# Probabilities times values of the cross attention: from fp32 matmuls to three fp16 products of high and low parts

## The chip, the cores and the metric

The kernel runs on one core of one Trainium2 chip. The metric is the device time of one execution in microseconds (us). Before the change two runs gave 828.41 and 826.72 us, a median of 827.57 us.

Five engines work side by side, each through its own instructions in order, and they wait for each other on semaphores. PE (TensorE) multiplies, DVE (VectorE) and ACT (ScalarE) read its results from PSUM, POOL (GpSimd) works between buffers in SBUF alone, and SP issues most of the DMAs.

## The reference

A decoder layer on x of 8 x 128 x 512: x plus self attention of the normed x (128 heads), plus cross attention of the normed result to a context of 8 x 128 x 512 (32 query heads, 8 key and value heads, head size 16, rotary positions), plus a base layer with eight gated low rank experts of the normed result. The change is in these lines of the cross attention:

```
v = jnp.repeat(v, N_REP, axis=1)
scores = jnp.einsum('bhqd,bhkd->bhqk', q, k) * scale
probs = jax.nn.softmax(scores, axis=-1)
ctx = jnp.einsum('bhqk,bhkd->bhqd', probs, v)
```

## The kernel before

The program spells out each engine's instructions by hand. Self attention fills the first three quarters of the span. The last quarter, from about 640 us, is the cross attention and the expert layer, written as one software pipeline over 32 **units**. A unit `u` is one of the 8 batches `b = u // 4` and one of four groups of 8 query heads `t = u % 4`. Every engine runs the same loop `for u in range(FIRST, ...)` with `b, r = (u + 1) // 4, (u + 1) % 4`. In step `u` of the loop the different parts of the pipeline work on different units:

- PE: `turn(u+2)` and `x_back(u-2)` (transposes, L1788 and L1839), then the long work of that step (below), then `x_rough(u+2)` (scores for the row maxima, L1798), `x_max_turn(u+1)`, `x_scores(u)` (scores by key, L1817) and `x_weigh(u-1)` (L1832), which multiplies the exponentials `XPT` with the values `xvz`. A column of ones beside the values gives the sums of the softmax.
- ACT: `turned_out(u+2)` (KQ, L1013), small reads of the step, `x_exps(u, 0)` (L1005), `x_out(u-1)` (OW, L1047), `x_exps(u, 1)`, and in the steps with r = 1 last the copy `query_high` (qst, L1055).
- DVE: the row maxima `x_max` (L1311), `x_outputs(u-1)` (division by the sums, L1321 and L1325), and the norms, gates and residual sums of the step.
- POOL: only a few pieces. In r = 0 it adds the bias (L810), in r = 1 it makes the low part of the queries (L817), in r = 2 it computes an inverse square root (L787, `inverse(1, ...)`) and spreads the keys (L828 to L831), in r = 3 another inverse square root (L787, `inverse(2, b - 1)`). This last one waits for the variance that DVE computes at the very end of its own step with r = 3 (`norm_stats(2, b - 1)`, L1288 to L1290). In six early steps POOL also makes low parts of weights (`split_low`, L798 and L801).

The long work on PE is the projection of the outputs in r = 3 (L1501, 12 matmuls) with a `norm_turn` (four transposes, L1849), the query projection in r = 0 (L1501, 12), the base layer and experts in r = 1 (L1740, 12, and L1747) with another `norm_turn`, and only the short gate product in r = 2 (L1501, 12 of 136 columns) with the transposes of the outputs (L1864). `XPT` has two buffers, picked by `u % 2`; the output of `x_weigh` goes to one PSUM bank.

The self attention already multiplies its probabilities in the way that the change brings to the cross attention: an fp16 copy `Ph` on ACT (L938), a low part `Pl` on POOL (L656), and 12 fp16 matmuls (L1654). `x_exps` and `x_weigh` of before are:

```
if u >= 2:
    act.wait_ge(s_xo, u - 1)
nc.scalar.activation(XPT[:, u % 2, h], PS[:, 4 + h, :], ACT.Exp).then_inc(s_ex, 1)
...
pe.wait_ge(s_ex, 2 * u + 2)
for g in range(2):
    for h in range(2):
        r = 32 * (2 * g + h)
        last = mm(PS[r:r + 32, o_bank(u), 0:2 * S], xvz[:, b, 2 * t + g, :], XPT[:, u % 2, h, 2 * g * S:2 * (g + 1) * S],
                  start=True, stop=True)
```

Of the kernel before, what the change touches and what calls it, by code (L numbers as in the profile page):

```python
# [7 lines left out]
F32 = mybir.dt.float32  # L8
F16 = mybir.dt.float16
# [5 lines left out]
P = 128  # L15
# [97 lines left out]
def build(nc, x, ctxT, pos, wdkr, wup, wqr, wo, xwq, xwkv, xwo, bw, ag, lb, bb, out):  # L113
    es = ExitStack()
    with es:
# [7 lines left out]
        def sb(name, shape, dt=F32):  # L123
            n = size[dt]
            for s in shape[1:]:
                n *= s
            at = top[0]
            top[0] = at + (n + 63) // 64 * 64
            return nc.alloc_sbuf_tensor_at(name, shape, dt, offset=at)
# [74 lines left out]
        assert top[0] <= os_at + 2 * GH * S * 4  # L204

        top[0] = end1 - 4 * KT * TOK * 2
        Pl = sb("Pl", [P, B, GH * S], F16)
        U = sb("U", [P, KT, TOK])
        SU = sb("SU", [P, TOK])
# [13 lines left out]
        CTh = sb("CTh", [P, KT, TOK], F16)  # L223
        CTl = sb("CTl", [P, KT, TOK], F16)

        top[0] = phase
        rt = sb("rt", [P, 2, DM])
        Wxh = sb("Wxh", [P, KT, DM], F16)
# [1 line left out]
        kst = sb("kst", [P, 2, NKV, 2, XROW], F16)  # L230
        assert top[0] <= wraw_at
        top[0] = wraw_at
        xvz = sb("xvz", [P, B, NKV, 32])
        assert top[0] <= w16_at
        top[0] = w16_at
        pn1 = sb("pn1", [P, 2, DM])
# [349 lines left out]
        def _(pool):  # L586
# [175 lines left out]
            for h in range(LATE, NH):  # L762
                p_low(job(h - 3))
                if h < TURN - 1:
                    late_rest(job(h).g + 1)
                if h == LATE:
                    values(G0 - 1, (G0 - 1) % 2)
                else:
                    late_values(job(h - 1))
                if h == TURN:  # L770
                    nc.gpsimd.memset(xvz[:], 0.0).then_inc(s_xvz, 1)
                if h == TURN + 1:
                    pool.wait_ge(s_kvo, B)
                    pool.wait_ge(s_xvz, 1)
                    nc.gpsimd.tensor_copy(xvz[:, :, :, 0:XVC], xv[:]).then_inc(s_xvz, 1)

            late_values(job(NH - 1))
            pool.wait_ge(s_q, 2 * NH)
# [12 lines left out]
            def split_low(n, k):  # L791
# [8 lines left out]
                pool.wait_ge(s_xw, done[0])  # L800
                nc.gpsimd.tensor_tensor(l, w, h, ALU.subtract).then_inc(s_xl, 1)  # L801

            for u in range(FIRST, LAST):
                b, r = (u + 1) // KT, (u + 1) % KT
                if r == 0 and 0 <= b - 2 < B:
                    v = b - 2
                    if v == 0:
                        pool.wait_ge(s_ffn, 80)
                    pool.wait_ge(n_xn[2], v + 1)
                    nc.gpsimd.tensor_tensor(xs[:, v, :], xs[:, v, :], bias[:], ALU.add).then_inc(s_xb, 1)  # L810
                if r == 1 and 0 <= b + 1 < B:

                    v = b + 1
                    pool.wait_ge(s_qst, 2 * v + 1)
                    q = qr[:].rearrange("p (h d) -> p h d", d=XD_)
                    part = [qst[:, v % 2, :, XD_ * i:XD_ * (i + 1)] for i in range(3)]
                    nc.gpsimd.tensor_tensor(part[2], q, part[0], ALU.subtract).then_inc(s_xqr, 1)  # L817
                if r == 2:
                    inverse(1, b + 2)
                if r == 2 and 0 <= b + 2 < B:  # L820

                    v = b + 2
                    if v >= 2:
                        pool.wait_ge(s_xt, KT * (v - 1))
                    pool.wait_ge(s_kvr, v // 4 + 1)
                    k = krc[:, v, :, None, :].to_broadcast([P, NKV, 2, XD_])
                    part = [kst[:, v % 2, :, :, XD_ * i:XD_ * (i + 1)] for i in range(3)]
                    nc.gpsimd.tensor_copy(part[0], k).then_inc(s_kst, 1)  # L828
                    nc.gpsimd.tensor_copy(part[2], k)
                    pool.wait_ge(s_kst, 2 * v + 1)  # L830
                    nc.gpsimd.tensor_tensor(part[1], k, part[0], ALU.subtract).then_inc(s_kst, 1)  # L831
                for n, k in LOWS_AT.get(u, ()):
                    split_low(n, k)
                if r == 3:
                    inverse(2, b - 1)

        @block.scalar
        def _(act):
# [161 lines left out]
            def x_exps(u, h):  # L1000
                if 0 <= u < NU:
                    act.wait_ge(s_st, 2 * u + h + 1)
                    if u >= 2:
                        act.wait_ge(s_xo, u - 1)
                    nc.scalar.activation(XPT[:, u % 2, h], PS[:, 4 + h, :], ACT.Exp).then_inc(s_ex, 1)  # L1005

            def turned_out(u):
                if 0 <= u + 2 < NU:
# [49 lines left out]
            for u in range(FIRST, NU):  # L1058
# [16 lines left out]
                x_exps(u, 0)  # L1075
                x_out(u - 1)
                x_exps(u, 1)
                if r == 1 and 0 <= b + 1 < B:
                    query_high(b + 1, 0)
                if u == FIRST + 2:  # L1080
# [411 lines left out]
        def _(pe):  # L1492
# [329 lines left out]
            def x_weigh(u):  # L1822

                b, t = u // KT, u % KT
                if 1 <= u < NU - 1:
                    pe.wait_ge(s_xon, u)
                pe.wait_ge(s_ex, 2 * u + 2)
                pe.wait_ge(s_xvz, 2)
                for g in range(2):
                    for h in range(2):  # L1830
                        r = 32 * (2 * g + h)
                        last = mm(PS[r:r + 32, o_bank(u), 0:2 * S], xvz[:, b, 2 * t + g, :], XPT[:, u % 2, h, 2 * g * S:2 * (g + 1) * S],  # L1832
                                  start=True, stop=True)
                last.then_inc(s_xo, 1)

            def x_back(u):
# [172 lines left out]
```

## Time and profile before

| What | Value |
|---|---|
| median of the runs | 827.57 us |
| the profiled execution, its own time | 826.78 us |
| its span in the trace | 824.5 us |
| mean granted clock of PE over the span | 0.998 |
| PE, DVE, ACT, POOL busy | 793.0, 628.6, 582.7, 590.9 us |

The span is what the trace covers, from its first to its last record; the execution's own time is 2.3 us longer. Busy time is a sum over the whole span. What an engine's time is worth in one stretch has to be read from that stretch: which engine waits there, and for whom. The names in the trace are the program's, with the line of the source (L1832 is `x_weigh`, L1005 is `x_exps`). An instruction of PE on fp32 operands has two records in the trace.

### The profile page before, as it was taken

How to read it: one execution, taken by the hardware profiler on the slowest of the kernel's cores; microseconds unless marked ns; L12 is line 12 of the kernel's file. 1: busy time of each engine (PE TensorE's matmuls, PEld its weight loads, DVE VectorE, ACT ScalarE, POOL GpSimd, SP SyncE). 2: the span in 40 equal slices, each digit the busy share in tenths (PEclk: the TensorE clock that was granted, in tenths of full speed). 3: DMA queues.
4: the chain of work that ended last, by engine and by line, in shares of the span. 5: the costliest groups of instructions: out<-in, count | busy, mean ns of one | idle time of the engine just before them, and what ended most of it. 6: DMA issues, size and time to landing. Idle time of an engine off the chain costs nothing.

```text
span 824.5 us, 17894 instructions
## 1 busy us (share of the span) xinstructions
PE 793.0 (96%) x5641; PEld 391.9 (48%) x5641; DVE 628.6 (76%) x1190; ACT 582.7 (71%) x1072; POOL 590.9 (72%) x535
## 2 busy tenths in 40 slices
PE   5999999999999999999999999999999899999987
PEld 3464444444444444444444444444444444555444
DVE  6766676676677788776788876778878888888766
ACT  8757777777777777777777777778765655666551
POOL 7967999999988888887888887878655634222111
PEclk9999999999999999999999999999999999999999
DMA  9344355533434333343333344352321000000001
GB/s 344 124 172 142 93 142 161 162 98 89 104 107 120 90 79 93 89 128 100 100 81 97 83 119 107 92 158 63 88 61 48 27 2 2 14 14 13 18 15 39
DMA packets 52176, 75.80 MB, mean 92 GB/s; under 512 B 10256, under 2 KB 34096, under 8 KB 51616
## 3 DMA queue, kind: packets, MB, share of 16 engines
q1 hardware_dynamic: 52128, 75.23, 32.8%
q8 instruction: 22, 0.36, 0.2%
q14 instruction: 26, 0.21, 0.1%
HBM read 38.69 MB, written 19.40 MB: 70 GB/s over the span
## 4 chain that ended last, share of the span: by engine, by line
PE 87%; DVE 4%; ACT 3%; issue 2%; SPq 2%; DMA 1%; POOL 0%; DVEq 0%; ACTq 0%
PE PS L1567 40%; PE PS L1639 7%; PE PS L1606 7%; PE PS L1640 7%; PE PS L1501 6%; PE PS L1654 5%; PE PS L1740 2%; PE PS L1832 2%; PE PS L1679 1%; PE PS L1798 1%; PE PS L1616 1%; PE PS L1688 1%; PE PS L1839 1%; PE PS L1817 1%; PE PS L1849 1%
## 5 line engine op out<-in xcount | busy, mean ns | idle before, releaser
L1567 PE MATMUL PS<-XTh,W 128*128 128x512 f16 x1024 | 346.0, 379 | 0.0
L656 POOL TENSOR_TENSOR Pl<-PR,Ph 128x512 f16<-128x512 f32 x254 | 285.8, 1156 | 28.4 <-ACT Ph L938 28.4
L931 ACT ACTIVATE PR<-PS 128x512 f32<-128x512 f32 x256 | 152.8, 597 | 131.7 <-PE PS L1640 124.9
L1125 DVE TENSOR_REDUCE mneg<-PS 128x4 f16<-128x512 f32 x256 | 171.6, 685 | 35.3 <-PE PS L1606 33.4
L1567 PE MATMUL PS<-XTl,W 128*128 128x512 f16 x512 | 193.6, 378 | 0.0
L1113 DVE SCALAR_TENSOR_TENSOR QS<-PS,QC 64x512 f16<-64x512 f32 x256 | 175.5, 685 | 20.8 <-ACT QC L848 16.7
L848 ACT ACTIVATE QC<-PS 64x512 f16<-64x512 f32 x256 | 150.7, 589 | 9.2 <-PE PS L1567 4.3
L1567 PEld LDWEIGHTS PS<-XTh,W 128*128 128x128 f16 x1024 | 96.6, 97 | 118.8 <-issue 25.9
L938 ACT ACTIVATE Ph<-PR 128x512 f16<-128x512 f32 x256 | 139.3, 617 | 0.0
L1606 PEld LDWEIGHTS PS<-KC,QC 112*128 112x128 f16 x1024 | 78.4, 97 | 63.5 <-issue 2.7
L1606 PE MATMUL PS<-KC,QC 112*128 112x128 f16 x1024 | 99.4, 219 | 0.9 <-ACT QC L848 0.8
L1639 PE MATMUL PS<-QC,KC 113*128 113x512 f16 x256 | 97.7, 382 | 1.3 <-DMA QC<-mT 1.2
L1640 PE MATMUL PS<-QS,KS 128*128 128x512 f16 x256 | 97.2, 380 | 0.0
L631 POOL TENSOR_TENSOR W<-Wraw,wscale 128x1024 f16<-128x1024 f32 x30 | 56.8, 1893 | 46.5 <-PE PS L1567 42.1
L1194 DVE TENSOR_SCALAR mT<-PS 16x128 f16<-16x128 f16 x64 | 13.6, 212 | 77.7 <-PE PS L1616 77.6
L1567 PEld LDWEIGHTS PS<-XTl,W 128*128 128x128 f16 x512 | 49.8, 97 | 46.3
L637 POOL TENSOR_TENSOR W<-Wraw,W 128x1024 f16<-128x1024 f32 x30 | 63.9, 2131 | 2.4
L787 POOL TENSOR_TENSOR rstd<-rstd,power 128x1 f32<-128x1 f32 x16 | 8.8, 553 | 74.3 <-DVE rstd L1290 74.3
L635 POOL TENSOR_TENSOR Wraw<-Wraw,wscale 128x1024 f32<-128x1024 f32 x30 | 56.7, 1891 | 0.2
L1200 DVE COPY OS<-PS 128x512 f32<-128x512 f32 x64 | 44.3, 692 | 4.1 <-PE PS L1654 2.2
L1311 DVE TENSOR_REDUCE xm<-PS 128x4 f16<-128x512 f32 x64 | 41.0, 683 | 2.0 <-PE PS L1798 2.0
L1654 PE MATMUL PS<-Ph,Vg 128*32 128x512 f16 x512 | 41.3, 383 | 0.0
(236 smaller groups left out, 1034.1 us busy)
## 6 DMA issues: line engine op xcount, KB each, us to landing
Wraw<-in_wqr SPq DMA_DIRECT2D x32, 512.0 KB, 4.8
QS<-QC SPq DMA_DIRECT2D x64, 256.0 KB, 3.2
head_outputs<-OS SPq DMA_DIRECT2D x256, 40.0 KB
q_content_parts<-stg SPq DMA_DIRECT2D x12, 256.0 KB, 2.9
k_content_parts<-stg SPq DMA_DIRECT2D x12, 256.0 KB, 3.1
QC<-q_content_parts SPq DMA_DIRECT2D x116, 24.0 KB
KC<-k_content_parts SPq DMA_DIRECT2D x29, 96.0 KB
xs<-in_x SPq DMA_DIRECT2D x8, 256.0 KB, 4.8
```

Of the source, the lines that this page charges most:

```text
L637: nc.gpsimd.tensor_tensor(Wl[:, par], Wraw[:, par], Wh[:, par], ALU.subtract).then_inc(s_ws, 1)
L656: nc.gpsimd.tensor_tensor(Pl[:, 4 * j.s + b], PR[:, b], Ph[:, 4 * j.s + b], ALU.subtract).then_inc(s_pl, 1)
L848: nc.scalar.activation(QC[0:RD, j.p, j.s, 2 * c + h, :], PS[RD * h:RD * (h + 1), bQ[c], :], ACT.Copy, scale=1 / WS).then_inc(s_qh, 1)
L931: nc.scalar.activation(PR[:, b, :], PS[:, bB[b % 2], :], ACT.Exp, scale=ATT_SCALE).then_inc(s_e, 1)
L938: nc.scalar.activation(Ph[:, 4 * j.s + b, :], PR[:, b, :], ACT.Copy).then_inc(s_ph, 1)
L1113: nc.vector.scalar_tensor_tensor(QS[0:RD, j.p, j.s, i, :], PS[RD * h:RD * (h + 1), bQ[c], :], 1 / WS, QC[0:RD, j.p, j.s, i, :], ALU.mult, ...
L1125: nc.vector.tensor_reduce(mneg[:, j.p, j.s, :, b], PS[:, bA[b % 2], :].rearrange("p (j k) -> p j k", j=GH), AX.X, ALU.max, negate=True).th ...
L1567: last = mm(PS[:, bQ[c], :], wt[:, j.w, k, c * P:(c + 1) * P], xt[:, k, sl], start=(i == 0), stop=(i == 3 * KT - 1))
L1606: last = mm(PS[:, bA[i % 2], h * S:(h + 1) * S], QC[0:MROW, j.p, j.s, h, i * S:(i + 1) * S], kc(j.k)[0:MROW, b * S:(b + 1) * S], start=Tru ...
L1639: mm(to, kc(j.k)[0:MROW + 1, b * S:(b + 1) * S], QC[0:MROW + 1, j.p, j.s, :, i * S:(i + 1) * S], start=True, stop=False)
L1640: mm(to, KS[:, b * S:(b + 1) * S], QS[:, j.p, j.s, :, i * S:(i + 1) * S], start=False, stop=True).then_inc(s_b, 1)
L1654: last = mm(PS[32 * b:32 * (b + 1), bO, :], Vg[:, j.p, part, 4 * j.s + b, :], probs[:, 4 * j.s + b, :], start=(n == 0), stop=(n == 2))
```

## The change

Only the product of probabilities and values in the cross attention is changed. ACT copies each half of the exponentials to fp16 (`XPh`, new function `x_highs`), POOL subtracts the copy from the original and writes the difference as fp16 (`XPl`, new function `x_lows`), and the values are kept as an fp16 pair in `xvz`, made once. `x_weigh` then adds three fp16 products, high by high, high values' low part by high, and low by high: 12 matmuls of 256 columns in place of 4 in fp32. PE waits for `XPl` only ahead of the third product. `x_exps(u)` now waits for the subtraction of unit u - 2 and no longer for its product.

```diff
-        xvz = sb("xvz", [P, B, NKV, 32])
+        xvz = sb("xvz", [P, 2, B, NKV, 32], F16)
...
+        XPh = sb("XPh", [P, 2, 2, REP * S], F16)
+        XPl = sb("XPl", [P, 2, 2, REP * S], F16)
...
-                    nc.gpsimd.tensor_copy(xvz[:, :, :, 0:XVC], xv[:]).then_inc(s_xvz, 1)
+                    nc.gpsimd.tensor_copy(xvz[:, 0, :, :, 0:XVC], xv[:]).then_inc(s_xvz, 1)
+                    pool.wait_ge(s_xvz, 2)
+                    nc.gpsimd.tensor_tensor(xvz[:, 1, :, :, 0:XVC], xv[:], xvz[:, 0, :, :, 0:XVC], ALU.subtract).then_inc(s_xvz, 1)
...
+            def x_lows(u):
+                if 0 <= u < NU:
+                    for h in range(2):
+                        pool.wait_ge(s_ph, 4 * NH + 2 * u + h + 1)
+                        if u == 0 and h == 0:
+                            pool.wait_ge(s_pv, NH)
+                        if u >= 2:
+                            pool.wait_ge(s_xo, u - 1)
+                        nc.gpsimd.tensor_tensor(XPl[:, u % 2, h], XPT[:, u % 2, h], XPh[:, u % 2, h], ALU.subtract).then_inc(s_pl, 1)
...
             for u in range(FIRST, LAST):
                 b, r = (u + 1) // KT, (u + 1) % KT
+                x_lows(u - 1)
...
                     if u >= 2:
+                        act.wait_ge(s_pl, pool_lows(NH - 1, 3) + 2 * (u - 2) + h + 1)
+                    nc.scalar.activation(XPT[:, u % 2, h], PS[:, 4 + h, :], ACT.Exp).then_inc(s_ex, 1)
+
+            def x_highs(u, h):
+                if 0 <= u < NU:
+                    act.wait_ge(s_ex, 2 * u + h + 1)
+                    if u >= 2:
                         act.wait_ge(s_xo, u - 1)
-                    nc.scalar.activation(XPT[:, u % 2, h], PS[:, 4 + h, :], ACT.Exp).then_inc(s_ex, 1)
+                    if u == 0 and h == 0:
+                        act.wait_ge(s_pv, NH)
+                    nc.scalar.activation(XPh[:, u % 2, h], XPT[:, u % 2, h], ACT.Copy).then_inc(s_ph, 1)
...
                 x_exps(u, 0)
                 x_out(u - 1)
                 x_exps(u, 1)
+                x_highs(u, 0)
+                x_highs(u, 1)
                 if r == 1 and 0 <= b + 1 < B:
                     query_high(b + 1, 0)
...
-                pe.wait_ge(s_ex, 2 * u + 2)
-                pe.wait_ge(s_xvz, 2)
-                for g in range(2):
-                    for h in range(2):
-                        r = 32 * (2 * g + h)
-                        last = mm(PS[r:r + 32, o_bank(u), 0:2 * S], xvz[:, b, 2 * t + g, :], XPT[:, u % 2, h, 2 * g * S:2 * (g + 1) * S],
-                                  start=True, stop=True)
+                pe.wait_ge(s_ph, 4 * NH + 2 * u + 2)
+                pe.wait_ge(s_xvz, 3)
+                for n, (probs, part) in enumerate(((XPh, 0), (XPh, 1), (XPl, 0))):
+                    if n == 2:
+                        pe.wait_ge(s_pl, pool_lows(NH - 1, 3) + 2 * u + 2)
+                    for g in range(2):
+                        for h in range(2):
+                            r = 32 * (2 * g + h)
+                            last = mm(PS[r:r + 32, o_bank(u), 0:2 * S], xvz[:, part, b, 2 * t + g, :],
+                                      probs[:, u % 2, h, 2 * g * S:2 * (g + 1) * S], start=(n == 0), stop=(n == 2))
```

How the new instructions stand among the old ones matters, since each engine keeps to its order. POOL in the second half of the cross attention, from the inverse square root of a step with r = 2 over r = 3, 0 and 1 to the next one of r = 2, before (a row is source line, operation, written tile <- read tiles, shape, and the semaphores waited for: `var_ready2` is the variance that DVE sends at the end of its step, `normed2` the normed rows, `xq_high` ACT's copy of the queries):

```order
L787 TENSOR_TENSOR rstd<-rstd,power 128x1 [waits var_ready1]
L828 CAST kst<-krc 128x16x16 [waits k_roped,kq_turned]
L829 CAST kst<-krc 128x16x16
L831 TENSOR_TENSOR kst<-krc,kst 128x16x16 [waits xk_parts]
L787 TENSOR_TENSOR rstd<-rstd,power 128x1 [waits var_ready2]
L810 TENSOR_TENSOR xs<-xs,bias 128x512 [waits normed2]
L817 TENSOR_TENSOR qst<-qr,qst 128x32x16 [waits xq_high]
```

and the same stretch of the change, where the source lines are shifted (`p_high` is ACT's copy of the exponentials):

```order
L795 TENSOR_TENSOR rstd<-rstd,power 128x1 [waits var_ready1]
L849 CAST kst<-krc 128x16x16 [waits k_roped,kq_turned]
L850 CAST kst<-krc 128x16x16
L852 TENSOR_TENSOR kst<-krc,kst 128x16x16 [waits xk_parts]
L821 TENSOR_TENSOR XPl<-XPT,XPh 128x512 [waits xo_ready,p_high] x2
L795 TENSOR_TENSOR rstd<-rstd,power 128x1 [waits var_ready2]
L821 TENSOR_TENSOR XPl<-XPT,XPh 128x512 [waits xo_ready,p_high] x2
L831 TENSOR_TENSOR xs<-xs,bias 128x512 [waits normed2]
L821 TENSOR_TENSOR XPl<-XPT,XPh 128x512 [waits xo_ready,p_high] x2
L838 TENSOR_TENSOR qst<-qr,qst 128x32x16 [waits xq_high]
L821 TENSOR_TENSOR XPl<-XPT,XPh 128x512 [waits xo_ready,p_high] x2
```

Each step now begins with two subtractions of the unit before, behind whatever POOL still had to do or to wait for in the step before: the pair of r = 0 stands behind the wait for `var_ready2`, the pair of r = 2 behind the wait for `xq_high`.

ACT from the score reads of a step with r = 1 to the read of KQ in r = 2, before:

```order
L998 ACTIVATE xmT<-PS 8x128 [waits xmax_in1,xmax_turned]
L1005 ACTIVATE XPT<-PS 128x512 [waits xo_ready,scores_by_key_ready]
L1047 ACTIVATE OW<-PS 128x256 [waits xo_turned,xo_ready]
L1005 ACTIVATE XPT<-PS 128x512 [waits xo_ready,scores_by_key_ready]
L1055 ACTIVATE qst<-qr 128x32x16 [waits kq_turned,xq_added]
L1013 ACTIVATE KQ<-PS 128x768 [waits scores_by_key_ready,kq_turned]
```

and of the change:

```order
L1019 ACTIVATE xmT<-PS 8x128 [waits xmax_in1,xmax_turned]
L1026 ACTIVATE XPT<-PS 128x512 [waits p_low,scores_by_key_ready]
L1077 ACTIVATE OW<-PS 128x256 [waits xo_turned,xo_ready]
L1026 ACTIVATE XPT<-PS 128x512 [waits p_low,scores_by_key_ready]
L1035 ACTIVATE XPh<-XPT 128x512 [waits xo_ready,xexp_ready] x2
L1085 ACTIVATE qst<-qr 128x32x16 [waits kq_turned,xq_added]
L1043 ACTIVATE KQ<-PS 128x768 [waits scores_by_key_ready,kq_turned]
```

Two copies stand between the second exponential and the copy of the queries and the read of KQ.

## Rows read from the trace of the kernel before

**Rows 1.** The page: busy time of the engines over the span.

```profile
PE 793.0 (96%) x5641; PEld 391.9 (48%) x5641; DVE 628.6 (76%) x1190; ACT 582.7 (71%) x1072; POOL 590.9 (72%) x535
```

**Rows 2.** Busy time by stretch, four steps each (instructions in brackets).

```profile
713.90:735.45 21.55, 20.77 (x182) 10.97 (x181) 19.14 (x53) 12.48 (x29) 4.82 (x8) 1.00 0.04 15
735.45:756.16 20.71, 19.94 (x181) 10.59 (x179) 17.41 (x50) 12.51 (x29) 4.85 (x8) 1.00 0.04 14
```

**Rows 3.** PE in order of time: start, us, line, tiles, shape, count.

```profile
400.60 0.65 PE L1654 MATMUL PS<-Ph,Vg 128*32 128x512 f16 x8
...
401.40 0.39 PE L1567 MATMUL PS<-XTh,W 128*128 128x512 f16 x1
```

**Rows 4.** ACT and POOL in order of time, self attention.

```profile
401.81 2.18 ACT L938 ACTIVATE Ph<-PR 128x512 f16<-128x512 f32 x4
...
596.21 4.50 POOL L656 TENSOR_TENSOR Pl<-PR,Ph 128x512 f16<-128x512 f32 x4 [2.89 <-ACT Ph L938]
```

**Rows 5.** PE in order of time, from r = 3 to r = 2.

```profile
737.88 0.60 PE L1849 MATMUL PS<-ident,pn 128*128 128x128 f32 x4
...
744.12 0.64 PE L1832 MATMUL PS<-XPT,xvz 128*32 128x256 f32 x8
744.69 0.33 PE L1754 MATMUL PS<-ident,low 128*128 128x128 f32 x1
...
749.99 0.39 PE L1817 MATMUL PS<-KQ 49*128 49x256 f16 x4
...
753.16 0.40 PE L1798 MATMUL PS<-KQ 48*128 48x128 f16 x8 [0.56 <-ACT KQ L1013]
...
754.55 0.64 PE L1832 MATMUL PS<-XPT,xvz 128*32 128x256 f32 x8
```

**Rows 6.** DVE in order of time, around the end of r = 3.

```profile
744.50 0.15 DVE L1290 TENSOR_SCALAR rstd<-mv 128x1 f32<-128x1 f32 x1
...
746.41 0.55 DVE L1297 TENSOR_SCALAR pn<-xs,mv,rstd 128x512 f32<-128x512 f32 x1
```

**Rows 7.** POOL in order of time, r = 3, 0, 1.

```profile
744.74 0.55 POOL L787 TENSOR_TENSOR rstd<-rstd,power 128x1 f32<-128x1 f32 x1 [9.12 <-DVE rstd L1290]
747.04 1.27 POOL L810 TENSOR_TENSOR xs<-xs,bias 128x512 f32<-128x512 f32 x1 [1.75 <-DVE pn L1297]
752.49 1.16 POOL L817 TENSOR_TENSOR qst<-qr,qst 128x512 f16<-128x512 f32 x1 [4.18 <-ACT qst L1055]
```

**Rows 8.** ACT in order of time, end of r = 1.

```profile
751.78 0.63 ACT L1055 ACTIVATE qst<-qr 128x512 f16<-128x512 f32 x1
752.30 0.81 ACT L1013 ACTIVATE KQ<-PS 128x768 f16<-128x768 f16 x1
```

**Rows 9.** POOL and PE in order of time: a weight split, the last steps.

```profile
670.14 1.16 POOL L801 TENSOR_TENSOR bwl<-bw_raw,bwh 128x512 f16<-128x512 f32 x1
...
802.48 0.64 PE L1832 MATMUL PS<-XPT,xvz 128*32 128x256 f32 x8
...
802.86 0.55 POOL L787 TENSOR_TENSOR rstd<-rstd,power 128x1 f32<-128x1 f32 x1 [14.41 <-DVE rstd L1290]
```

**Rows 10.** PE's longest wait of this stage, then by half microsecond: busy, clock, DMA.

```profile
684.45 0.63 PE L1849 MATMUL PS<-ident,pn 128*128 128x128 f32 x4 [1.76 <-DVE rt L1121]
...
685.00:685.50 0.50, 0.50 (x12) 0.92 0.00 0
685.50:686.00 0.50, 0.50 (x5) 0.50 0.00 0
...
688.50:689.00 0.50, 0.50 (x9) 0.66 0.00 0
```

**Rows 11.** One DVE instruction beside POOL's bias near the end, and in a plain piece.

```profile
812.46 1.27 POOL L810 TENSOR_TENSOR xs<-xs,bias 128x512 f32<-128x512 f32 x1 [0.66 <-DVE pn L1297]
...
812.89 0.87 DVE L1349 TENSOR_SCALAR ex<-ex,mx 128x8 f32<-128x8 f32 x1
...
742.96 0.23 DVE L1349 TENSOR_SCALAR ex<-ex,mx 128x8 f32<-128x8 f32 x1
```

More of the change, by code:

```diff
@@ L206, in build @@
         top[0] = end1 - 4 * KT * TOK * 2
+        xpart_at = top[0]
         Pl = sb("Pl", [P, B, GH * S], F16)
@@ L224, in build @@
         CTl = sb("CTl", [P, KT, TOK], F16)
+        top[0] = xpart_at
+        XPh = sb("XPh", [P, 2, 2, REP * S], F16)
+        XPl = sb("XPl", [P, 2, 2, REP * S], F16)
+        assert top[0] <= xpart_at + B * GH * S * 2
         top[0] = phase
@@ L770, in _ @@
                 if h == TURN:
-                    nc.gpsimd.memset(xvz[:], 0.0).then_inc(s_xvz, 1)
+                    nc.gpsimd.memset(xvz[:].rearrange("p a b h c -> p (a b h c)").bitcast(F32), 0.0).then_inc(s_xvz, 1)
                 if h == TURN + 1:
```

## The prediction, made before the changed kernel ran

> **What bounds the kernel now.** The page comes first: PE is busy for 793.0 of 824.5 us, ACT and POOL for some 70% [rows 1]. That says PE is the engine to watch, but it is a mean over two stages, and the change touches only the last one. So I read next the busy time by stretch there, in pieces of four steps (one batch). In a plain piece of 20.71 us PE is busy for 19.94 us, DVE for 17.41, ACT for 12.51 and POOL for 4.85 [rows 2]. PE sets the pace, DVE is close behind it, and POOL looks as if it had 16 us to spare. The order of time then shows why that spare time is not free: POOL spends it standing in front of particular instructions. It waits 9.12 us for DVE's variance before the inverse square root of r = 3, which starts at 744.74, and 4.18 us for ACT's copy of the queries in r = 1 [rows 7]. What is queued behind these waits cannot run during them. The reader should see one more thing: POOL gets the variance at 744.65, after PE has begun the product of unit and values of the *next* step (744.12) [rows 5, 6]. DVE is about a step behind PE.
>
> **PE's own gain.** Today a product takes 0.57 us (744.12 to 744.69) [rows 5], in all 32 x 0.57 = 18 us. The same form in self attention, 12 fp16 matmuls of 512 columns (8 of high parts stand in the row), takes 0.80 us from its first start to the next matmul [rows 3]; half the columns give at most 0.40 us, and as a small transpose shares that time I take 0.32. The gain is 0.25 us, 8 us in all, and it is the upper bound: where the read of OW follows an exponential on ACT, that and not PE is last. I count 0.08 us a unit, 2.5 us.
>
> **ACT's copies.** Four take 2.18 us [rows 4], 0.54 us each, 1.08 us a unit. In r = 3, 0 and 1 what ACT does next has more slack than that, since PE has 2.6 us or more of long work to do. In r = 2 it has none: PE already waits 0.56 us for KQ [rows 5], which follows the copy of the queries directly, and that the second exponential [rows 8]. There the copies go on the path in full.
>
> **POOL's subtractions.** Four take 4.50 us [rows 4], so a pair takes 1.12 + 1.16 = 2.3 us. Placed by their queue (the unit's step is that of the loop in which PE multiplies):
>
> - *Step r = 0, wait A.* The pair stands behind the inverse square root: 744.74 + 0.55 + 2.3 = 747.6 [rows 7]. PE has done its first two products by 744.35 and waits to 747.7; the product ends at 747.8, not 744.69: +3.1 us. Where DVE had more to do in the piece it is 2.7. I take 2.9. DVE does not make this up: from the transposes at 737.88 to the variance it works nearly without a gap, and the next round of it hangs on PE again.
> - *Step r = 1.* The pair follows the bias, which follows the normed rows (746.41 [rows 6]) and these the late product. Counted from the end of that product, back transposes 0.9, division 0.7, normed rows 0.5, bias 1.3 and the pair 2.3 give 5.7 us; PE needs it 5.85 us after (744.69 to 750.32 and two products). No wait, with 0.15 us to spare.
> - *Step r = 2, wait B.* KQ comes 1.08 us later, so the rough scores start at 754.24 and the product at 755.63. The queries' copy also ends 1.08 late, at 753.5, POOL's query part at 754.7, the pair at 757.0, the product at 757.2 in place of 755.12 (754.55 and the same 0.57) [rows 5, 7, 8]: +2.1 us. The copies are in that number.
> - *Step r = 3.* The pair ends 1 us before PE wants it. No wait.
>
> **The count.** Wait A occurs in six steps (7, 11, ... 27): first 2.1 (less to wait for there), then 5 x 2.9, in all 16.6. Wait B occurs in steps 1, 5, ... 25. Six of them give 12.6; in step 5 a weight split of 1.1 + 1.16 us [rows 9] stands in the queue too, so that one gives 4.0; step 29 has no queries and costs 0.6: 17.2. Splits in steps 7 and 9 delay two more pairs by 1.6 and 1.5: 3.1. At the end, the variance lands at 802.8, the inverse at 803.4 [rows 9]; the pair of unit 30 ends at 805.7, then back transpose, division, normed rows, bias (809.2) and the pair of unit 31 (811.5). PE's last product ends at 811.7 in place of 803.05: +8.6. The last query projection falls away in step 27, where PE has nothing to gain from it any more: +0.9. Against it stand an fp32 output product of 0.86 us in two of the steps, now inside wait A (-1.7), and PE's gain (-2.5). Sum: 16.6 + 17.2 + 3.1 + 8.6 + 0.9 - 1.7 - 2.5 = **+42 us**.
>
> The values' low part is one more subtraction of 1,088 columns at about 593 us, some 2.4 us at the rate of [rows 4]. It lies in the 2.89 us that POOL stood idle before 596.21 [rows 4]; without that cover it would cost its 2.4.
>
> **The clock.** PE's longest idle time in this stage is 1.76 us. After it the granted clock fell from 1.00 to 0.50 (1.2 GHz) at about 685.5 and rose again at about 688.8 [rows 10]: 3.3 us at half speed, about 1.6 us of work lost. Waits A and the last one are longer than that idle time, and the long work of r = 1 follows them, which is on the path. I take seven such falls, 11.2 us, less the 1.6 that today's fall costs: **+10 us**. Bounds: nothing (idle times of 0.56 us in each piece leave the clock at 1.00 [rows 2, 5]), and 7 more falls at wait B, +7, since half of each would be hidden. The Trainium skill ("TensorE: Matmul & The Clock Gate", HAM oscillation) names waits between groups of matmuls of 3 to 5 us as what brings the lower rate each time; the row shows it here after 1.76 us, so the measurement is the stricter of the two, and by the page's figure alone waits A would sit at the edge.
>
> 826.8 (the profiled execution, 0.8 under the median) + 42 + 10 = **879 us**.
>
> **The rivals.**
>
> - *The waits come, the clock holds.* For it: the clock is 1.00 over the pieces shown, though PE idles in each [rows 2, 5]. Against it: one fall after only 1.76 us [rows 10]. 826.8 + 42 = 869.
> - *POOL and DVE hold each other up.* A DVE instruction of 0.23 us took 0.87 us while POOL's bias ran [rows 11]. POOL would run 9 us more per piece, and DVE's queries (0.69) fall on a pair in each r = 1: 0.5 us, and up to two more such meetings, 0.5 to 1.5 us in 7 pieces: 879 + 9 = 888. The Trainium skill ("SBUF — State Buffer", Who interferes with whom) says that the two share a pair of ports as an exclusive lock, held for a whole instruction; the row agrees.
> - *Only ACT's delay shows*: the pairs are ready in time, since PE itself comes late enough. It costs 8 x 1.08 - 2.5 = +6: 833, within 2%. Against it: POOL's start in r = 0 is set by the variance, and that moves with PE.
> - *Not slower.* If both copies and pairs are hidden, the shorter product is all that is left: 827 - 8 = 819. The point that decides is POOL's pair in r = 0: it must end before 744.3, so it would have to run ahead of the inverse square root and not behind it. The order says behind.
>
> **How the numbers follow.** I count 2% (16.5 us) as what can be told from no change. Forecast, waits and clock: 0.52, 879 (866 to 892). Clock holds: 0.20, 869. Ports: 0.12, 888. ACT alone: 0.10, 833. Not slower: 0.04, 819; faster by over 2% would need all of the product's 18 us gone: 0.02, counted with it. The range 852 to 894 takes in the first three with their bounds and leaves out the last ones and waits that are half as long (848). Slower 0.84, same 0.14, faster 0.02.
>
> **What would show it.** Right: PE idle before the third product in r = 0 for about 3 us, released by POOL's `XPl`; about 1.3 us in r = 2, after a wait for KQ of about 1.6; POOL's pair directly behind the inverse square root; pieces of 25 to 27 us in place of 21; granted clock 0.50 for some 3 us after each long wait. Wrong: PE without idle time before its third product, or pieces that keep 21 us. The forecast fails if the variance reaches POOL earlier relative to PE than before, or if PE's lateness hides the pairs.

## The result and the profile after

Two runs of the changed kernel gave 893.41 and 895.35 us, a median of 894.38 against 827.57 before: 1.0807 times as long (95% interval 1.0785 to 1.0829), so slower by 66.8 us. The forecast was 879; its range, 852 to 894, ended 0.4 us below what was measured. The profiled execution is the one of 893.41 us, with a span of 891.7 us and a mean granted clock of 0.958.

The page of the changed kernel, busy time over the span, answers to [rows 1]:

```profile
PE 815.6 (91%) x5769; PEld 404.8 (45%) x5769; DVE 644.5 (72%) x1190; ACT 615.9 (69%) x1136; POOL 667.9 (75%) x600
```

POOL has 77 us more, ACT 33, and PE's 22.6 are mostly the same work at a lower clock, as shown below. The stretches of four steps that answer to [rows 2], each from one of POOL's inverse square roots of r = 3 to the next (length, then busy time and instructions of PE, PEld, DVE, ACT and POOL, granted clock, DMA share, GB/s):

```profile
723.65:751.22 27.57, 23.23 (x212) 12.32 (x212) 21.06 (x53) 16.90 (x37) 14.51 (x16) 0.94 0.03 11
751.22:778.52 27.30, 21.50 (x205) 11.60 (x203) 19.73 (x51) 17.37 (x38) 14.50 (x15) 0.94 0.04 12
778.52:808.53 30.01, 25.10 (x195) 12.91 (x195) 18.84 (x50) 16.68 (x36) 14.35 (x16) 0.77 0.03 10
808.53:835.18 26.65, 19.32 (x179) 10.43 (x179) 16.86 (x45) 15.94 (x35) 12.53 (x11) 0.86 0.03 11
```

A piece takes 27 to 30 us where it took 21, and no engine is busy for all of it. POOL in order of time shows why; it answers to [rows 7]:

```profile
751.22 0.55 POOL L795 TENSOR_TENSOR rstd<-rstd,power 128x1 f32<-128x1 f32 x1 [7.59 <-DVE rstd L1322]
751.73 2.26 POOL L821 TENSOR_TENSOR XPl<-XPT,XPh 128x512 f16<-128x512 f32 x2
756.57 1.27 POOL L831 TENSOR_TENSOR xs<-xs,bias 128x512 f32<-128x512 f32 x1 [2.57 <-DVE pn L1329]
757.79 2.81 POOL L821 TENSOR_TENSOR XPl<-XPT,XPh 128x512 f16<-128x512 f32 x2
763.51 1.16 POOL L838 TENSOR_TENSOR qst<-qr,qst 128x512 f16<-128x512 f32 x1 [2.90 <-ACT qst L1085]
764.62 2.27 POOL L821 TENSOR_TENSOR XPl<-XPT,XPh 128x512 f16<-128x512 f32 x2
```

Each pair stands directly behind the piece that waited: behind the inverse square root (r = 0), the bias (r = 1) and the queries' low part (r = 2). PE in the same steps, which answers to [rows 5]:

```profile
751.22 0.40 PE L1867 MATMUL PS<-XPh,xvz 128*32 128x256 f16 x8
...
754.05 0.29 PE L1867 MATMUL PS<-XPl,xvz 128*32 128x256 f16 x4 [2.43 <-POOL XPl L821]
...
760.66 0.29 PE L1867 MATMUL PS<-XPl,xvz 128*32 128x256 f16 x4 [0.37 <-POOL XPl L821]
...
764.18 0.40 PE L1830 MATMUL PS<-KQ 48*128 48x128 f16 x8 [1.59 <-ACT KQ L1043]
...
766.95 0.41 PE L1867 MATMUL PS<-XPl,xvz 128*32 128x256 f16 x4 [0.97 <-POOL XPl L821]
```

The third product starts when POOL's pair ends: 751.73 + 2.26 = 753.99, and 754.05. The waits of PE from 640 us on, summed (waiting line, releaser: us in total, times, longest), before and after:

```profile
PE PS L1798 <- ACT KQ L1013: 5.5, 9, 1.1
```

```profile
PE PS L1867 <- POOL XPl L821: 34.8, 17, 4.3
PE PS L1830 <- ACT KQ L1043: 15.2, 11, 2.2
```

These two sums are 44.5 us more than the one of before (34.8 + 15.2 - 5.5). Beside the waits there is slower work. Three stretches of after with their clock, columns as above:

```profile
780.00:786.50 6.50, 5.14 (x22) 2.59 (x23) 3.06 (x8) 2.78 (x6) 3.28 (x4) 0.51 0.00 0
...
794.00:801.00 7.00, 7.00 (x38) 3.28 (x39) 5.17 (x13) 4.29 (x10) 6.36 (x8) 0.53 0.00 0
858.50:872.50 14.00, 6.18 (x33) 3.20 (x33) 2.22 (x10) 2.98 (x7) 6.26 (x6) 0.51 0.00 1
```

The clock falls 14 times in this stage, for 3 to 14 us each. Added up by half microseconds, PE is at 1.2 GHz for 75 us, 57 of them busy; before it was 3.5 us, nearly all of them busy. So some 27 us of its work (half of 57, less 1.7) run beside the schedule, much of it inside steps in which PE would have waited anyway.

### The profile page after: what moved, and what is told of

It reads as the page before. It is cut to its first block, busy times and chain, and to the rows that moved or that the text cites. A ratio compares the mean times of both kernels' runs of the same rounds, so it can differ in the third digit from the quotient of the medians.

```text
span 891.7 us, 18401 instructions
## 1 busy us (share of the span) xinstructions
PE 815.6 (91%) x5769; PEld 404.8 (45%) x5769; DVE 644.5 (72%) x1190; ACT 615.9 (69%) x1136; POOL 667.9 (75%) x600
## 4 chain that ended last, share of the span: by engine, by line
PE 68%; issue 13%; POOL 11%; DVE 4%; ACT 1%; SPq 1%; DMA 1%; POOLq 0%; DVEq 0%; ACTq 0%
PE PS L1599 36%; POOL XPl L821 8%; PE PS L1671 6%; PE PS L1638 6%; PE PS L1672 6%; PE PS L1686 4%; PE PS L1533 2%; PE PS L1711 1%; PE PS L1648 1%; PE PS L1720 1%; DMA QC<-mT 1%; PE PS L1558 1%; DVE QS L1145 1%; PE PS L1772 1%; DMA xs<-in_x 1%
## 5 line engine op out<-in xcount | busy, mean ns | idle before, releaser
L821 POOL TENSOR_TENSOR XPl<-XPT,XPh 128x512 f16<-128x512 f32 x64 | 75.5, 1201 | 10.4 <-ACT XPh L1035 10.2
L1867 PE MATMUL PS<-XPl,xvz 128*32 128x256 f16 x128 | 10.9, 330 | 34.8 <-POOL XPl L821 34.8
```

The source lines that it names most:

```text
L821: nc.gpsimd.tensor_tensor(XPl[:, u % 2, h], XPT[:, u % 2, h], XPh[:, u % 2, h], ALU.subtract).then_inc(s_pl, 1)
```

## The experiments

In the diffs `-` is the changed kernel unless another is named. The time before, in the runs beside them, was 826.7 to 827.7 us.

**1. Hold the clock up.** PE repeats the first product (a group is 4 matmuls) ahead of the real one, and does the gate product twice more. The result stays as it is, since each group starts its sum anew.

```diff
+                for _ in range(again):
+                    parts(bank, Ah2[:, v % 2], Al2[:, v % 2], agh, agl, 0, AG, (n_tl[2], v + 1))
...
+            def fill(u):
+                return {4: 24, 7: 24, 31: 40}.get(u, 8 if u % 4 == 0 else 20 if u % 4 == 2 and u >= 6 else 0)
...
+                    for _ in range(fill(u) if n == 0 else 0):
+                        for g in range(2):
+                            for h in range(2):
+                                r = 32 * (2 * g + h)
+                                mm(PS[r:r + 32, o_bank(u), 0:2 * S], xvz[:, part, b, 2 * t + g, :],
+                                   probs[:, u % 2, h, 2 * g * S:2 * (g + 1) * S], start=True, stop=True)
...
-                        gate(v, bF[1])
+                        gate(v, bF[1], 2)
```

> The changed kernel, but PE fills part of its waits: it repeats the first of the three products up to 24 times (40 in the last unit) where POOL's low part is late, and the gate product twice more where KQ is late. The results are overwritten by equal ones, and no wait is taken away. Theory: beside the waits for POOL, the changed kernel (893.4 us profiled) loses time at half clock, much more of it than the 10 us predicted. Then the granted clock stays near 1.00 and the time falls to 868 to 875, the waits alone. Rival: the excess over the prediction is longer waits (ports, ACT), and the clock is hidden by them: 885 or more, with the clock at 1.00 all the same.

Measured: 884.77 us, clock 0.994, 10 us at half speed. The last fill was made too long. It ran at half clock and ended 3.6 us after the pair that it was to bridge (857.6):

```profile
853.89 7.45 PE L1873 MATMUL PS<-XPh,xvz 128*32 128x256 f16 x160 [1.08 <-ACT XPh L1035]
```

So the clock is worth 9.6 us (894.38 - 884.77), and 13 if the 3.6 of that overrun are taken off; this is one run. That is at the edge of the rival's range, and far from the first theory's. The waits without the clock are the larger part: 884.77 - 3.6 - 827.7 = 53.5 us, where the forecast had 42.

**2. The product alone.** The exponentials are written as fp16 at once, with no copies and no subtractions; the third product reads the high parts again. The waits go with them: `x_exps(u)` waits for the product of unit u - 2, as before the change.

```diff
-                    nc.scalar.activation(XPT[:, u % 2, h], PS[:, 4 + h, :], ACT.Exp).then_inc(s_ex, 1)
+                    nc.scalar.activation(XPh[:, u % 2, h], PS[:, 4 + h, :], ACT.Exp).then_inc(s_ex, 1)
...
-                x_lows(u - 1)
...
-                x_highs(u, 0)
-                x_highs(u, 1)
...
-                for n, (probs, part) in enumerate(((XPh, 0), (XPh, 1), (XPl, 0))):
+                for n, (probs, part) in enumerate(((XPh, 0), (XPh, 1), (XPh, 0))):
```

> PE's part alone: ACT writes the exponentials as fp16 at once, with no copies and no subtractions, and the third product reads the same fp16 tile again (the low part of the probabilities is left out of the result). Theory: PE's product is 0.25 us shorter a unit, but the read of OW follows an exponential in many steps, so 2.5 us are gained of 8: 824 (823 to 826). Rival: all 8 us are gained: 819.

Measured: 826.62 us, median of 10 runs, ratio 0.9988 (0.9971 to 1.0004). PE's gain is 1.1 us, not 8, and cannot be told from none; it is a little above the first theory's range. Its time shows in where the next matmul starts:

```profile
743.53 0.51 PE L1864 MATMUL PS<-XPh,xvz 128*32 128x256 f16 x12
743.97 0.33 PE L1785 MATMUL PS<-ident,low 128*128 128x128 f32 x1
...
754.91 0.44 PE L1871 MATMUL PS<-ident,OW 128*128 128x128 f32 x2 [0.20 <-ACT OW L1078]
```

A unit's 12 matmuls take 0.44 us (743.53 to 743.97) where the four in fp32 took 0.57 (744.12 to 744.69 in [rows 5], ahead of the same transpose): 0.13 us less, half of the 0.25 forecast, 4.2 us in 32 units. Of these, 1.4 us go into waits for ACT's `OW` (2.4 us in 8 such waits, 1.0 in 2 before), and some more into other waits.

**3. No subtractions**, with ACT's copies as in the change.

```diff
-                x_lows(u - 1)
...
-                        act.wait_ge(s_pl, pool_lows(NH - 1, 3) + 2 * (u - 2) + h + 1)
+                        act.wait_ge(s_ph, 4 * NH + 2 * (u - 2) + h + 1)
...
-                for n, (probs, part) in enumerate(((XPh, 0), (XPh, 1), (XPl, 0))):
-                    if n == 2:
-                        pe.wait_ge(s_pl, pool_lows(NH - 1, 3) + 2 * u + 2)
+                for n, (probs, part) in enumerate(((XPh, 0), (XPh, 1), (XPh, 0))):
```

> The changed kernel without POOL's subtractions: the third product reads the fp16 copy a second time, so the low part is left out of the result; ACT's copies and PE's 12 matmuls stay. Theory: all that is left is ACT's 1.08 us in each step r = 2 (8.6 us) less PE's gain of 2.5: 833 us (830 to 837), clock near 1.00. Rival: ACT's copies carry a larger part of the loss (they delay KQ and all behind it): 845 or more.

Measured: 844.64 us (one run), at the rival's 845 and not in the theory's range. ACT's copies cost 844.64 - 826.62 = 18 us, twice what I had counted. PE's waits from 640 us on:

```profile
PE PS L1829 <- ACT KQ L1042: 16.5, 11, 2.2
```

The product alone has 6.1 in 10. Two of the waits in order of time:

```profile
740.98 0.40 PE L1829 MATMUL PS<-KQ 48*128 48x128 f16 x8 [1.59 <-ACT KQ L1042]
...
794.75 0.61 PE L1829 MATMUL PS<-KQ 48*128 48x128 f16 x8 [1.78 <-ACT KQ L1042]
```

The first is wait B's 0.56 + 1.03, as forecast. The second stands in a step of r = 0 that has no query projection any more; before, the same wait was 0.76. Half speed follows the first and begins within the second:

```profile
743.00:746.50 3.50, 3.48 (x14) 1.58 (x12) 3.33 (x13) 2.90 (x7) 0.29 (x1) 0.51 0.03 5
794.00:801.50 7.50, 6.75 (x43) 3.34 (x44) 4.15 (x13) 4.33 (x9) 1.81 (x2) 0.54 0.06 24
```

That is not so behind every such wait. Of the five waits of 1.59 us in this execution (at 694.47, 717.54, 740.98, 763.78 and 785.18) only the second and the third have a fall behind them, at 719.0 and 743.0; the others leave the clock at 1.00.

**4. The same with PE's idle time filled** by the gate product twice more in r = 2.

> The kernel without subtractions (844.6 us; the low part is left out of the result), and in addition PE repeats the gate product twice where it waits for KQ in the steps r = 2 from step 9 on; the repeats are overwritten by equal results. Theory: of the 18 us that ACT's copies cost beyond the product alone (826.6), half is the granted clock that falls behind the 1.59 us wait for KQ, five or six times 1 to 1.5 us: 837 to 840. Rival: all of it is KQ's lateness, and the repeats change nothing: 843 to 846.

Measured: 839.92 us (ratio 1.0152, 1.0135 to 1.0169), in the first theory's range and 4.7 below experiment 3. The mean clock alone does not bear the theory out: it is 0.983 in the profiled execution, against 0.987 in experiment 3. It fell three times ahead of the first filled step, step 9 (from about 652.5, 669.5 and 690 on), within or behind waits of 2.16, 1.78 and 1.77 us that experiment 3 has too, there without a fall. The comparison unit by unit does: the scores of unit 13 start 0.5 us later in experiment 3 than here, those of unit 14 by 1.7, of unit 18 by 3.1 and of unit 28 by 4.4, and these steps lie behind experiment 3's falls at 719, 743 and 794. So about 4 of the 18 us are half speed that the fills took away, in one execution of each kernel. The waits for KQ fell to 7.0 us in 9, but that is the fill's doing, since the gate product stands ahead of them.

**5. The copies behind KQ.** Experiment 3 with the copies of a unit moved into the next step, right behind the read of KQ (those of the last unit behind the loop).

```diff
                 turned_out(u)
+                x_highs(u - 1, 0)
+                x_highs(u - 1, 1)
...
-                x_highs(u, 0)
-                x_highs(u, 1)
```

> The kernel without POOL's subtractions (the third product reads the high parts again, so the result lacks the probabilities' low part) and with ACT's two copies of a unit moved from the end of its step to the next step, right behind the read of KQ. With the copies ahead of KQ it gave 844.6 us, the product alone 826.6. Theory (the copies cost because they stand ahead of the read of KQ, with PE's idle time and the clock's falls that follow): 828 to 833 us, PE's waits for KQ back at 5 to 6 us. Rival (ACT has no room for 1.08 us more in a step, wherever they stand): 840 us or more, with PE waiting for other reads of ACT in place of KQ.

Measured: 830.84 us (1.0045, 1.0029 to 1.0061), the first theory. The same copies, in the same number, cost 4.2 us there (830.84 - 826.62) and 18 ahead of KQ. PE's waits are those of before again:

```profile
PE PS L1831 <- ACT KQ L1042: 5.5, 9, 1.1
PE PS L1873 <- ACT OW L1076: 2.6, 9, 0.7
```

**6. POOL's order.** The whole change, but each unit's subtractions stand in the step that computes it: first in the step where r is not 2, and behind the keys where r = 2.

```diff
-                x_lows(u - 1)
+                if r != 2:
+                    x_lows(u)
...
+                if r == 2:
+                    x_lows(u)
                 for n, k in LOWS_AT.get(u, ()):
```

> The changed kernel with one thing moved: POOL subtracts a unit in the step in which ACT copies it, in r = 3 ahead of the inverse square root, in r = 1 ahead of the queries' low part, in r = 0 ahead of the bias, and in r = 2 behind the spread keys, in place of at the start of the next step. The same work on every engine. Theory: the loss is the place in POOL's queue, so waits A and B and the clock's falls go: 836 us (832 to 842). Rival: POOL's 2.3 us a unit are the cost wherever they stand (the pair then delays the variance's inverse, the queries or the keys as much): 860 or more.

Measured: 860.5 us (1.0398, 1.0353 to 1.0443). The order costs 894.38 - 860.5 = 33.9 us, the largest single part, but my 836 was far off, and 860 is where the rival began: 16 us stay above experiment 3 with PE hardly waiting for `XPl` (4.2 us in 3 times).

**7 and 8. One wait at a time.** Only the pair of r = 3 ahead of the inverse square root, against wait A:

```diff
-                x_lows(u - 1)
+                if r != 0:
+                    x_lows(u - 1)
...
                 if r == 3:
+                    x_lows(u)
                     inverse(2, b - 1)
```

> The changed kernel with wait A alone taken away: in r = 3 POOL subtracts ahead of the inverse square root, all other pairs keep their places. Theory: A (about 3.1 us in seven steps), the long wait in the last unit (8.6) and the clock's falls behind them are the larger part of the 34 us by which the full reordering beat the changed kernel (894.4 to 860.5): 866 to 872. Rival: the two waits feed each other, so one alone gives little: above 880.

Measured: 873.51 us, 20.9 less than the change and just above the theory's range. And only the pair of r = 1 ahead of the queries' low part, against wait B:

```diff
-                x_lows(u - 1)
+                if r != 2:
+                    x_lows(u - 1)
+                if r == 1:
+                    x_lows(u)
```

> The changed kernel with POOL's part of wait B alone taken away: in r = 1 POOL subtracts ahead of the queries' low part. Theory: only the 0.97 us of that wait, seven times, 3.2 in place of it in step 5, and perhaps half of their clock's falls go; KQ stays late by ACT: 882 to 887. Rival: POOL's queue in r = 1 is what sets the next steps too: 878 or less.

Measured: 881.36 us, 13.0 less, just below the theory's range. Together 33.9, what experiment 6 gave at once: neither wait hides much of the other. That the sums meet to a tenth is chance, since both are single runs, and experiment 6 also moves the pairs of r = 0 and r = 2.

**9. Subtractions that nobody reads.** Experiment 6, but PE's third product reads the high parts and waits for no subtraction.

> The reordered kernel, with POOL's subtractions still made, but not waited for by PE: the third product reads the fp16 copy again (the low part is left out of the result). It stands between the kernel without subtractions (844.6 us) and the reordered one (860.5). Theory: the 16 us between them are not PE's waits, which nearly vanished in the reordered kernel, but POOL's load: DVE instructions that stand still while POOL works, and POOL's other pieces that come later. So 856 to 860. Rival: PE's waits for the low part, though short, set off the clock: 845 to 850.

Measured: 854.34 us (1.0318, 1.0290 to 1.0346), between the two ranges. Of the 16 us above experiment 3, about 10 stay though PE waits for POOL's pairs nowhere. The size of the other 6 is not sure: the intervals of experiments 6 and 9 lie apart by less than 0.1%, and the slowest of the four runs here (857.87, the profiled one) is above the fastest there (857.22). What PE waits for more is DVE:

```profile
PE PS L1833 <- ACT KQ L1046: 16.5, 11, 2.2
PE PS L1885 <- DVE rt L1156: 4.8, 3, 2.8
PE PS L1536 <- DVE Al L1338: 3.3, 2, 2.6
PE PS L1789 <- DVE low L1386: 2.1, 2, 1.7
```

10.2 us in the three with DVE, where experiment 3 has 3.8 (1.8, 1.6 and 0.4). The longest chain to PE, first DVE, then POOL, then PE:

```profile
704.54 1.18 DVE L1373 TENSOR_TENSOR eq<-low 128x64 f32<-128x64 f32 x1
...
706.75 1.20 DVE L1375 TENSOR_TENSOR gt<-gt,eq 128x64 f32<-128x64 f32 x1
```

```profile
703.31 2.33 POOL L821 TENSOR_TENSOR XPl<-XPT,XPh 128x512 f16<-128x512 f32 x2 [0.90 <-ACT XPh L1038]
```

```profile
710.69 1.87 PE L1536 MATMUL PS<-Wxh,Ah 128*128 128x512 f16 x4 [2.59 <-DVE Al L1338]
```

The first comparison (0.22 us before) ends with POOL's pair. The next two DVE instructions, the second of them shown, end with the two instructions of a weight split that POOL does right behind the pair, `Al` comes late by them, and PE waits 2.59 us and goes on at half clock. Unit by unit most of the loss lies there: the scores of unit 11 already start 10.1 us later than in experiment 3, those of unit 31 by 13.7, and the weight splits stand in the steps ahead of unit 11. DVE's instructions from 700 to 820 us, grouped (busy us, mean ns), before:

```profile
L1297 DVE TENSOR_SCALAR pn<-xs,mv,rstd 128x512 f32<-128x512 f32 x10 | 5.4, 544 | 1.1 <-POOL rstd L787 0.7 <-DVE O L1325 0.2
...
L1437 DVE TENSOR_TENSOR qr<-rt 128x512 f32<-128x512 f32 x4 | 2.8, 693 | 0.1
...
L1338 DVE TENSOR_TENSOR eq<-low 128x64 f32<-128x64 f32 x7 | 1.5, 218 | 0.0
```

and here:

```profile
L1332 DVE TENSOR_SCALAR pn<-xs,mv,rstd 128x512 f32<-128x512 f32 x9 | 7.7, 856 | 0.2
...
L1373 DVE TENSOR_TENSOR eq<-low 128x64 f32<-128x64 f32 x5 | 5.9, 1174 | 0.0
...
L1472 DVE TENSOR_TENSOR qr<-rt 128x512 f32<-128x512 f32 x4 | 4.4, 1093 | 0.1
```

**10. Fills in place of subtractions.** Experiment 9, with a POOL instruction that reads nothing (the added wait keeps the fills in order):

```diff
-                        nc.gpsimd.tensor_tensor(XPl[:, u % 2, h], XPT[:, u % 2, h], XPh[:, u % 2, h], ALU.subtract).then_inc(s_pl, 1)
+                        pool.wait_ge(s_pl, pool_lows(NH - 1, 3) + max(2 * u + h - 1, 0))
+                        nc.gpsimd.memset(XPl[:].rearrange("p a h s -> p (a h s)")[:, 1024 * h:1024 * (h + 1)], 0.0).then_inc(s_pl, 1)
```

> The good order on POOL with nobody reading the subtractions gave 854.3 us, and without them 844.6. Here each subtraction is replaced by a fill of 1,024 fp16 elements with zeros, which reads nothing and lasts about 0.96 us in place of 1.13, at the same place behind the same waits (the probabilities' low part is left out of the result). Theory (the 9.7 us are DVE instructions held up by a POOL instruction that reads): 845 to 848 us, the comparison eq (two inputs in SBUF) back at 0.22 us from 1.17, and less waiting of PE for DVE. Rival (POOL's being busy, and the place of its other pieces behind that work, is what costs): 852 to 856 us, even if single DVE instructions get shorter.

Measured: 846.88 us (1.0246, 1.0201 to 1.0291), 7.5 less than experiment 9 and 2.2 above experiment 3. PE's waits for DVE in the three places of experiment 9 are back at 3.9 us, the first of them the longest:

```profile
PE PS L1886 <- DVE rt L1157: 3.2, 1, 3.2
```

So a queue nearly as full costs little in this order, no more than the spread of the runs, and most of the 10 us go when POOL's instruction reads nothing and is shorter. But `pn` is held up here as well, and `ex` (a scalar form too) with the two instructions queued behind it, while they run free away from a fill:

```profile
L1333 DVE TENSOR_SCALAR pn<-xs,mv,rstd 128x512 f32<-128x512 f32 x10 | 9.6, 961 | 0.4 <-DVE O L1361 0.2
...
L1374 DVE TENSOR_TENSOR eq<-low 128x64 f32<-128x64 f32 x6 | 2.5, 416 | 0.0
```

```profile
790.61 1.08 DVE L1370 TENSOR_SCALAR ex<-low,mx 128x8 f32<-128x8 f32 x1
790.75 0.94 DVE L1373 TENSOR_TENSOR gt<-low 128x64 f32<-128x64 f32 x1
790.89 0.81 DVE L1374 TENSOR_TENSOR eq<-low 128x64 f32<-128x64 f32 x1
```

They all end at 791.7, where POOL's fill ends (789.83 + 1.84). The queries' sum `qr` is long too (1.38 us), but it meets the bias there, which reads. Part of the theory failed with that: the saving came without `pn` getting shorter. A fill is also shorter than a subtraction, 983 against 1,195 ns in the mean; no run separates its length from its not reading, and which of the held instructions carries the cost stays open. The Trainium skill ("SBUF — State Buffer", Who interferes with whom) tells the forms apart: a DVE instruction with two inputs in SBUF is held only by a POOL instruction that reads, scalar forms in their fast mode by any. These rows agree.

**11. Order and clock.** Experiment 6 with the gate product twice more.

> The order with each unit's subtractions in its own step gave 860.5 us with 43.5 us of PE's time at half clock; here the gate product of each r = 2 is done twice more (its result is the same), which fills PE's idle time there. If half of what is left over the kernel before in that order is the clock, 850 to 855 us, with a mean clock above 0.985. If the idle times themselves are what costs and the clock only follows them, 858 to 862 us.

Measured: 857.66 us (1.0376, 1.0334 to 1.0417) against 860.5, clock 0.981 against 0.976, at half speed for 32 us against 41 (the 43.5 of the expectation counts half microseconds that were low only in part as whole ones). The intervals overlap, so this run decides nothing; the repeats fill idle time in r = 2 alone.

**12. Both orders mended.** Experiment 6 with the copies behind KQ as in experiment 5.

> The whole change with both orders mended: each unit's subtractions in a place of their own in POOL's queue, and ACT's copies behind the read of KQ in the next step. The order of POOL alone gave 860.5 us. Theory (ACT's place and POOL's place add up): 843 to 850 us. Rival (copies that come a step later make POOL's pairs late again, so PE waits for XPl for what it no longer waits for KQ): 856 us or more. Neither theory has it below the kernel before.

Measured: 869.31 us (1.0508, 1.0485 to 1.0530), the rival, and worse than the order of POOL alone. KQ is in time again, but POOL now waits for the copies, and what stands behind them waits with it. PE's waits, and POOL in order of time:

```profile
PE PS L1872 <- POOL XPl L821: 14.1, 12, 1.8
PE PS L1825 <- POOL qst L839: 7.3, 8, 1.0
PE PS L1835 <- ACT KQ L1046: 5.7, 9, 1.1
PE PS L1889 <- DVE rt L1158: 5.6, 5, 3.4
```

```profile
754.03 2.27 POOL L821 TENSOR_TENSOR XPl<-XPT,XPh 128x512 f16<-128x512 f32 x2 [3.81 <-ACT XPh L1038]
756.27 1.15 POOL L839 TENSOR_TENSOR qst<-qr,qst 128x512 f16<-128x512 f32 x1
```

No version of the change beat the kernel before. The nearest, experiment 2, cannot be told from it and does not compute the low parts.

## Why the forecast came out short

The medians, put in a row, split the 66.7 us (894.38 - 827.7):

| Part | measured, from | forecast |
|---|---|---|
| the product alone | -1.1 (2 against before) | -2.5 |
| ACT's copies, with the clock behind their waits | +18.0 (3 - 2) | +8.6 |
| POOL's work in good order, unread | +9.7 (9 - 3) | 0 |
| PE waiting for it there | +6.2 (6 - 9), unsure | 0 |
| the order in POOL's queue, with its clock | +33.9 (change - 6) | 36.1 and most of the clock's 10 |

The order in which the parts are taken matters for the clock, which follows whatever waits are left. The table also shows that 879 came nearer to 894 than its parts deserved: the order in the queue was priced too high (46 against 33.9), and what stays in a good order far too low (8.6 - 2.5 = 6 against 32.8). The two errors cancel in part, which is luck.

- **The cause was right.** The two waits lie where the forecast had them: 2.43 us of idle time behind the inverse square root in r = 0, then 1.59 for KQ and 0.97 for `XPl` in r = 2 (forecast: about 3, 1.6 and 1.3). Experiments 7 and 8 show each by itself, and 6 both.
- **PE's gain** was taken down to 2.5 us from a bound of 8, with `OW` as the reason. It is 1.1, and `OW` is less than half of the reason: the product is shorter by 0.13 us and not by 0.25, since the 12 matmuls take 0.44 where halving those of 512 columns gave me 0.32, so the bound was 4.2, and waits for `OW` take 1.4 of it.
- **The step that failed: what the new work costs where PE does not wait for its result.** I said of r = 3, 0 and 1 that "what ACT does next has more slack than that", and priced POOL's instructions only by when their result is ready. Both were wrong. On ACT, the waits of r = 2 grew by about 1.03 each, as counted; but KQ was late by as much in steps 4 and 27, where PE has no long work and had waited 0.76 us already, and the clock fell behind waits of 1.59 us, which the forecast had only as a bound of +7. Together 18 us in place of 8.6: 10.4 in waits for KQ (16.5 - 6.1), the rest in other waits and at half clock, some 4 of it by experiment 4. On POOL, instructions whose result nobody waits for cost about 10 us where the sum had nothing, and 7.5 of them went with fills in their place: DVE's instructions are held up, and I had given that a chance of 0.12 as a rival with +9, not a place in the sum.
- **r = 1** was to have no wait, with 0.15 us to spare. The pair there took 2.81 us in place of 2.26, as DVE's `qr` falls on it, and PE waited 0.37. The same shows in the length of a piece: with the clock held up (experiment 1) the scores of unit 27 start 17.6 us further behind those of before than the scores of unit 15, 5.9 us per piece, where the two waits were to give 5.0.
- **The end** grew by 10.7 us between the scores of unit 31 and the last instruction, 8.6 forecast; the clock is at 0.51 in it.
- **The clock** was sized well by luck. It falls twice as often as I took (14 times, not 7) and stays down longer (3 to 14 us, not 3.3), but the lost work, 27 us, costs only 9.6 to 13 us in experiment 1, 10 forecast, since PE would have waited anyway in many of these steps. Nor does a wait settle it by its length: experiments 3 and 4 have equal waits with a fall behind them and without. The Trainium skill ("TensorE: Matmul & The Clock Gate", HAM oscillation) describes falls behind waits of 3 to 5 us; here some come behind waits of 1.59 us.
- **The values' low part** is hidden, as said: it took 2.3 us at 594.4, in POOL's idle time.
- **The rivals.** "Only ACT's delay shows" and "not slower" fell with PE's 34.8 us of waiting for `XPl`, "the clock holds" with the clock's rows. "POOL and DVE hold each other up" came in on top of the forecast and not in its place; its 888 is nearer to 894, but it too leaves ACT's copies at 8.6.

Still open: how the 10 us of POOL in good order divide among the DVE instructions held up, how much of them is POOL's reading and how much its length, how large PE's 6 us in that order really are, and what decides whether the clock falls behind a given short wait.

## What to carry to other kernels

Price an instruction added to an engine with idle time by three things, not one: when its result is ready, what stands behind it in its queue, and what its running holds up on the engine beside it. Here the arithmetic gain was 1 us, and the queue positions alone cost 34 on POOL and 14 on ACT, for the very same instructions. Where a wait already existed in the trace, however short (0.56 and 0.76 us here), a delay of 1.08 ahead of it lengthened it by 1.03; list all such waits of the stage, not only those of the step one has in mind. And check where an instruction waits before moving it: the copies behind KQ saved 14 us alone and cost 9 with POOL queued for them.

## What the runs showed of the hardware

- The granted clock fell to 0.51 (1.2 GHz) behind an idle time of 1.59 us in an otherwise busy stretch, with PE busy for 2.41 of the 4 us from 739 to 743 (experiment 3), and later stayed there for 7 us with PE busy for 6.75 of 7.5 us. Three other waits of 1.59 us in the same execution had no fall behind them, and waits of 2.16 and 1.78 us had none there and one each in the execution of experiment 4, which is the same kernel up to that point.
- With fills on POOL, which read nothing, DVE's fp32 scalar form `pn` took 961 ns in the mean in place of 544 (experiment 10). With subtractions on POOL a comparison of 64 elements took 1,174 ns in place of 218 (experiment 9).
- Twelve fp16 matmuls of 256 columns on 32 columns of the array take 0.44 us from their start to the next matmul's (experiment 2), and the four fp32 ones 0.57: at this shape three products of halves gain 0.13 us over one in fp32.
